# A four-layer graph network: degree norms moved to running totals, own rows added on VectorE, relation products with features on partitions

## The reference, cut to what matters

```
# layer 1: relation weights
xw   = einsum('ni,rio->rno', h, weight)            # 8 relations
msgs = relu(xw[edge_type, src] + bias)
out  = segment_sum(msgs, dst)
# layer 2: two of these, then two dense layers
xw   = h @ W                                        # (A+I): own row included
norm = dis[row] * dis[col]                          # dis = rsqrt(degree of the target side)
agg  = segment_sum(xw[row] * norm[:, None], col) + b
```

## Time and profile before

| | us |
|---|---|
| three runs, median | 9220.77 |
| three runs, lowest and highest | 9168.85, 9257.79 |
| the profiled execution: its own time | 9174.45 |
| the profiled execution: its span | 9172.8 |

### The profile page before, as it was taken

How to read it: one execution, slowest core, us unless ns; L and a number is a source line. 1 busy time by engine, 2 the same in 40 slices (tenths; PEclk the granted TensorE clock), 3 DMA queues, 4 the chain that set the end, 5 groups by cost and what they waited for, 6 DMA issues and landing times. The chain is left out here.

```text
span 9172.8 us, 117781 instructions
## 1 busy us (share of the span) xinstructions
PE 4151.0 (45%) x22767; PEld 3257.0 (36%) x22767; DVE 5226.7 (57%) x22501; ACT 2665.3 (29%) x6456; POOL 4913.5 (54%) x4624
## 2 busy tenths in 40 slices
PE   7004555556678888860003689700167523222000
PEld 1003333336667777760002578600056411111000
DVE  8766555559975666658861467522146544444544
ACT  0670000027632222223321356400022333333222
POOL 0007888864445555555557720166687355555466
PEclk9556665568877888885555799855589755555555
DMA  8893222248832222226654789611279522222333
GB/s 231 325 352 65 41 41 41 41 96 274 276 106 62 64 65 67 65 72 160 161 144 159 236 287 310 200 45 44 63 240 318 193 81 83 80 81 82 94 113 103
DMA packets 1124322, 1274.86 MB, mean 139 GB/s; under 512 B 220752, under 2 KB 933434, under 8 KB 1113735
## 3 DMA queue, kind: packets, MB, share of 16 engines
q1 hardware_dynamic: 924340, 976.35, 33.2%
q0 software_dynamic: 199904, 297.70, 13.6%
HBM read 680.87 MB, written 620.27 MB: 142 GB/s over the span
## 5 line engine op out<-in xcount | busy, mean ns | idle before, releaser
L627 POOL DMA_INDIRECT dense<-t_xs,gidx x784 | 764.9, 976 | 845.1 <-DVE gidx L1388 447.6
L1687 PE MATMUL ps<-w,dense 128*128 128x128 f32 x6272 | 976.4, 312 | 131.0 <-issue 128.4
L1687 PEld LDWEIGHTS ps<-w,dense 128*128 128x128 f32 x6272 | 868.9, 218 | 206.0 <-issue 167.2
L455 POOL DMA_INDIRECT g<-t_src,gidx x398 | 404.4, 1016 | 774.2 <-DVE keyr L489 653.2
L1408 DVE SCALAR_TENSOR_TENSOR dense<-xT 128x256 f32<-128x256 f32 x1568 | 543.9, 418 | 474.4 <-ACT xT L1843 336.4
L627 POOL DMA_INDIRECT dense<-t_y,gidx x392 | 373.3, 952 | 753.0 <-DVE gidx L1498 634.1
L473 POOL DMA_INDIRECT t_acc<-tot,sidx x392 | 641.1, 1635 | 141.8 <-issue 124.2
L757 ACT ACTIVATE dense<-dense,nbi,sc 128x128 f32<-128x128 f32 (+1 forms) x1580 | 624.7, 480 | 232.8 <-DVE nbi L1362 166.7
L1073 POOL DMA_INDIRECT g<-out_rows,gidx x392 | 371.0, 946 | 493.2 <-DVE didx L1544 363.6
L532 PE MATMUL ps<-ident,keyr 128*128 128x128 f32 x394 | 118.6, 399 | 1051.9 <-DVE seq L502 547.8
L565 POOL DMA_INDIRECT out_rows<-dense,sidx x392 | 384.8, 982 | 280.5 <-DVE dense L1593 167.8
(11 more groups left out here) (296 smaller groups left out, 12909.3 us busy)
## 6 DMA issues: line engine op xcount, KB each, us to landing
dense<-t_xs SPq DMA_DIRECT2D x78, 1320.0 KB
dense<-in_x SPq DMA_DIRECT2D x156, 640.0 KB
t_xs<-dense SPq DMA_DIRECT2D x98, 528.0 KB, 7.3
t_xs<-hb SPq DMA_DIRECT2D x78, 660.0 KB
t_sum<-dense SPq DMA_DIRECT2D x98, 512.0 KB
t_src<-dense SPq DMA_DIRECT2D x78, 640.0 KB
t_acc<-dense SPq DMA_DIRECT2D x78, 640.0 KB
dense<-t_acc SPq DMA_DIRECT2D x78, 640.0 KB
```

Source lines behind the costliest of these rows:

```text
L455: gp.indirect_dma_start(rows[:, p.k, c, :], None, table, bass.IndirectOffsetOnAxis(ap=gidx[:, p.k, c:c + 1], axis=0)) \
L627: gp.indirect_dma_start(rows[:, p.k, c, :], None, table, bass.IndirectOffsetOnAxis(ap=gidx[:, p.k, c:c + 1], axis=0)) \
L1687: i = nc.tensor.matmul(ps[:, o:o + P], xm[:, p.w, k, c * P:(c + 1) * P], w1[:, k, :], start=False, stop=(k == R - 1))
```

## The change

Three parts, and small things that go with them.

1. **E1.** The weights become the stationary side and the masked rows of both tiles move together: eight matmuls of 256 columns a pair. The result has features on partitions, so the bias is a column that ACT adds in its relu. PE then turns the two messages back (`turn_back`, lag 2), and the running totals read them from PSUM. The bias matmuls go.
2. **Layer 2's target norm.** E0 and the start of L0 compute on DVE the degree norm of each edge's target from a scan over run lengths (`normd`), with one small matmul and one square root on ACT. In E2, ACT multiplies every total by it (`e2_scaled`, lag 3) into a ring of its own, which SP stores; `run_sums` then waits for this copy in place of the store.
3. **L2.** DVE adds the own rows to the sums in place of scaling them; PE turns the result with ten transposes a block in place of twenty identity matmuls.
4. In **E3** the lag of the running totals behind the gathers goes from 3 to 5.

```diff
             def e1_sums(p):
-                v.wait_ge(E1["relu"].sem, E1["relu"].after(p.q + 1))
-                run_sums(v, R1, p, tot1, msg[:, p.w, 0, :], msg[:, p.w, 1, :], 2)
+                v.wait_ge(E1["back"].sem, E1["back"].after(p.q + 1))
+                run_sums(v, R1, p, tot1, *[ps[:, BACK[p.w] + c * P:BACK[p.w] + (c + 1) * P] for c in range(2)], 2)
...
             def products(p):
...
+                o = XW + p.w * 512
+                for k in range(R):
+                    i = nc.tensor.matmul(ps[:, o:o + 2 * P], w1[:, k, :], xm[:, p.w, k, :], start=(k == 0),
+                                         stop=(k == R - 1))
+                i.then_inc(E1["xw"].sem, 1)
+
+            def turn_back(p):
+                pe.wait_ge(E1["relu"].sem, E1["relu"].after(p.q + 1))
+                if needed(p.q - 1):
+                    pe.wait_ge(R1["second"].sem, R1["second"].after(p.q - 1))
                 for c in range(2):
-                    o = XW + p.w * 512 + c * P
-                    nc.tensor.matmul(ps[:, o:o + P], ones[0:1, :], b1b[0:1, :], start=True, stop=False)
-                    for k in range(R):
-                        i = nc.tensor.matmul(ps[:, o:o + P], xm[:, p.w, k, c * P:(c + 1) * P], w1[:, k, :],
-                                             start=False, stop=(k == R - 1))
-                i.then_inc(E1["xw"].sem, 1)
-
-            pair_loop(pe, (turn, 0), (products, 1))
+                    o = BACK[p.w] + c * P
+                    i = nc.tensor.transpose(ps[:, o:o + P], msg[:, p.w, c, :], ident[:, :])
+                i.then_inc(E1["back"].sem, 1)
+
+            pair_loop(pe, (turn, 0), (products, 1), (turn_back, 2))
...
             def e1_relu(p):
                 if needed(p.q - 1):
-                    a.wait_ge(R1["second"].sem, R1["second"].after(p.q - 1))
+                    a.wait_ge(E1["back"].sem, E1["back"].after(p.q - 1))
                 a.wait_ge(E1["xw"].sem, E1["xw"].after(p.q + 1))
-                nc.scalar.activation(msg[:, p.w, :, :], pair_of(XW + p.w * 512), ACT.Relu).then_inc(E1["relu"].sem, 1)
+                nc.scalar.activation(msg[:, p.w, :, :], pair_of(XW + p.w * 512), ACT.Relu, bias=b1c[:, :]) \
+                    .then_inc(E1["relu"].sem, 1)
...
+            def e2_scaled(p):
+                a.wait_ge(R2["second"].sem, R2["second"].after(p.q + 1))
+                if needed(p.n):
+                    a.wait_ge(R2["keep"][p.k].sem, R2["keep"][p.k].after(p.n * 16))
+                for c in range(2):
+                    i = nc.scalar.activation(scaled2[:, p.k, c, :], tot[:, p.k, c, :], ACT.Copy,
+                                             scale=normd[:, bass.ds(p.q * 2 + c, 1)])
+                i.then_inc(R2["scaled"].sem, 1)
+            pair_loop(a, (e2_root, 0), (e2_body, 1), (e2_scaled, 3))
...
             def enc_scale(r, u, p):
                 b = r * SLOTS + u
                 v.wait_ge(L2["lda"][u].sem, L2["lda"][u].after(r * 16 + 16))
-                nc.vector.tensor_tensor(ain2[u][0:p], ain2[u][0:p], norm_of(u, p, D), ALU.mult).then_inc(L2["scal"].sem, 1)
+                v.wait_ge(L2["h"].sem, L2["h"].after(b + 1))
+                nc.vector.tensor_tensor(ain2[u][0:p], ain2[u][0:p], hb[u][0:p, :, 0:D], ALU.add).then_inc(L2["scal"].sem, 1)
...
                 for k in range(K):
-                    nc.tensor.matmul(ps[:, k * P:k * P + p], ain2[u][0:p, k, :], ident[0:p, 0:p], start=True, stop=False)
-                    i = nc.tensor.matmul(ps[:, k * P:k * P + p], hb[u][0:p, k, 0:D], ident[0:p, 0:p], start=False, stop=True)
+                    i = nc.tensor.transpose(ps[:, k * P:k * P + p], ain2[u][0:p, k, :], ident[0:p, 0:p])
                 i.then_inc(L2["tr"].sem, 1)
...
-            pair_loop(v, (e3_ring, 0), (e3_sums, 3))
+            pair_loop(v, (e3_ring, 0), (e3_sums, 5))
```

```diff
+            nc.vector.tensor_scalar(ta[:, 1:T], cont[:, 1:T], 1.0, None, ALU.mult)
+            chain(nc.vector.memset(ta[:, 0:1], 1.0))
+            v.wait_ge(C0["turned"].sem, C0["turned"].after(2))
+            chain(nc.vector.tensor_copy(carried[:, 0:1], ps[:, 7 * 512:7 * 512 + 1]))
+            chain(nc.vector.tensor_tensor_scan(tb[:, :], ta[:, :], hcol[0][:, :], carried[:, 0:1], ALU.mult, ALU.add))
+            nc.vector.tensor_scalar(normd[:, :], tb[:, :], 1.0, None, ALU.add).then_inc(C0["v"].sem, 1)
+            v.wait_ge(C0["root"].sem, C0["root"].after(2))
+            chain(nc.vector.reciprocal(normd[:, :], normd[:, :]))
```

More of the change, by code:

```diff
@@ L307, in gnn @@
         TURN = (1 * 512, 4 * 512)
+        BACK = (0, 3 * 512)
         SUMS = 2 * 512
@@ L417, in gnn @@
         E0 = phase("edge", NPAIR, EN + "hot count", GA, EXTRA)
-        C0 = phase("target_degrees", 1, "v close root made shared turned carried keys kept")
+        C0 = phase("target_degrees", 1, "v close root made shared turned keys kept")
         SW = {"keep": [16 * len(range(k, NPAIR, RING)) for k in range(RING)]}
@@ L423, in gnn @@
                    {"ld": slots(16), "lda": slots(16), "sto": slots(16)})
-        E1 = phase("edge", NPAIR, "ring bn mv var std rs nb h tx txc masked xw relu", GP)
+        E1 = phase("edge", NPAIR, "ring bn mv var std rs nb h tx txc masked xw relu back", GP)
         R1 = phase("runs", NPAIR, "first second", SC)
@@ L428, in gnn @@
         E2 = phase("edge", NPAIR, "ring joined bn mv var std rs sc nb h", GP)
-        R2 = phase("runs", NPAIR, "first second", SW)
+        R2 = phase("runs", NPAIR, "first second scaled", SW)
         Z2 = phase("last_runs", 1, "made close total last:16")
@@ L640, in run_sums @@
             width = in0.shape[-1]
-            if needed(p.n):
+            if free == "scaled":
+                if needed(p.q - RING + 1):
+                    v.wait_ge(s["scaled"].sem, s["scaled"].after(p.q - RING + 1))
+            elif needed(p.n):
                 v.wait_ge(s[free][p.k].sem, s[free][p.k].after(p.n * (32 if per else 16)))
@@ L907, in keep_runs2 @@
             def keep_runs2(p):
-                sp.wait_ge(R2["second"].sem, R2["second"].after(p.q + 1))
+                sp.wait_ge(R2["scaled"].sem, R2["scaled"].after(p.q + 1))
                 sp.dma_start(t_run2[0:T * P, :].rearrange("(p t) f -> p t f", t=T)[:, bass.ds(p.q * 2, 2), :],
-                             tot[:, p.k, :, :]).then_inc(R2["keep"][p.k].sem, 16)
+                             scaled2[:, p.k, :, :]).then_inc(R2["keep"][p.k].sem, 16)
             pair_loop(sp, (clear(t_yacc, zrow[:, :, 0:H2], E2["h"]), 0), (keep_runs2, 1))
@@ L1304, in needs @@
                 vec.tensor_scalar(need[:, :], needf[:, :], 1.0, None, ALU.max)
+                chain(vec.memset(hcol[0][:, :], 1.0))
+                chain(vec.tensor_tensor_scan(normd[:, :], cont[:, :], hcol[0][:, :], 0.0, ALU.mult, ALU.add))
             def e0_between(pair):
@@ L1344, in _ @@
             v.wait_ge(C0["made"].sem, C0["made"].after(late[0] + 3))
+            late[0] += 3
             for n in range(2):
@@ L1446, in e2_sums @@
                 v.wait_ge(E2["h"].sem, E2["h"].after(p.q + 1))
-                run_sums(v, R2, p, tot, g[:, p.k, 0, :], g[:, p.k, 1, :], 0, "keep")
+                run_sums(v, R2, p, tot, g[:, p.k, 0, :], g[:, p.k, 1, :], 0, "scaled")
             run_start(v, Z2, tot)
             pair_loop(v, (e2_ring, 0), (e2_stats, 3), (e2_scales, 4), (e2_sums, 5))
-            run_close_vector(v, Z2, msg[:, 0, 0, :], D)
+            v.wait_ge(Z2["close"].sem, Z2["close"].after(1))
+            nc.vector.tensor_scalar(msg[:, 0, 0, :], ps[:, SUMS:SUMS + D], carried[:, 1:2], None, ALU.mult) \
+                .then_inc(Z2["total"].sem, 1)
             end_phase(v, VE)
@@ L1661, in conv0_mm @@
                 i.then_inc(L0["mm"].sem, 1)
+            nc.tensor.matmul(ps[:, 7 * 512:7 * 512 + 1], carry[:, :], normd[:, T - 1:T], start=True, stop=True) \
+                .then_inc(C0["turned"].sem, 1)
             node_loop(pe, (conv0_turn, 0), (conv0_mm, 1))
@@ L1703, in enc_turn @@
                 pe.wait_ge(L2["scal"].sem, L2["scal"].after(b + 1))
-                pe.wait_ge(L2["h"].sem, L2["h"].after(b + 1))
                 if needed(b):
@@ L1828, in conv0_first @@
                 relu_rows(a, p, ob_h[u], xin[u], sc[:, u, :], nbi[:, u, :]).then_inc(L0["h"].sem, 1)
+            a.wait_ge(C0["v"].sem, C0["v"].after(2))
+            nc.scalar.activation(normd[:, :], normd[:, :], ACT.Sqrt).then_inc(C0["root"].sem, 1)
             node_loop(a, (conv0_first, 0))
```

20 lines of the change are left out of this document (13 added, 7 removed).

## The result

Beside the kernel before in the same set of runs, the kernel after takes 8843.74 us (median of 4, 8766.52 to 8885.96) against 9194.81 (median of 4): ratio 0.9603, 95% interval 0.9512 to 0.9693. The forecast, 8760 us and faster by over 1%, came true in its total. By the medians the gain is 351 us; the profiled execution of after is the fastest of its four, and beside it the gain is 408 us. The parts of the forecast did not come true, and a later set of runs took the kernel before down to 8050 us. So there are two questions: where the 408 us between the two profiled executions (9174.45 and 8766.52) came from, and when they exist at all.

The account below looks back on a forecast made before the run. E1 was held by PE at 5.23 us a pair plus 455 us lost, mainly to slow stretches, L2 by DMA transfers from block 22. 9174.45 - 290 - 90 - 50 + 3 = 8747, given as 8760 us; range 8520 to 9110.

Parts of the forecast that it names:

- The floor of E1: E1: POOL's gathers and writes set 5.3 us a pair, 1060 us undisturbed, no gain on 1045 by itself.
- E1, -290: E1: 1060 us undisturbed plus 150 us of remaining loss gives 1210, minus 290 us (ends -420 and -40).
- a third of the loss: E1: of the loss to PE's slow stretches, between 20 and 400 us, 150 us was let stand.
- the first rival: The slow stretches vanish: E1 1080 us (-420), L2 -175, E3 -60, total 8522 us; chance 0.25.
- hidden at full clock: E1: DVE's wait for `turn_back` costs nothing, 3.7 + 0.3 us of PE against 5 us of DVE.
- L2, -90: L2: fewer PE records help only the first blocks; middle taken between nothing and at most 180 us.
- E3, -50: E3: the longer lag covers 5 us more of late gathers; minus 50 us, between none and 80.
- full recovery: E3: the upper bound of the longer lag's gain, 80 us, with POOL's floor at 2.49 us a pair.
- E2, +3: E2, L0, E0 and start together +3 us; E2's scaled copies hidden, its store about +1 at the end.
- Clock in L2: L2: transposes may bring PE to 1.2 GHz, a block 10.9 us over DMA's 9.67, +80, 8840 us; chance 0.06.
- Slower, POOL never pausing: E1: POOL hardly pauses, PE keeps crawling at 29.6 us a pair; 26 such pairs give 9317 us; chance 0.08.
- Density of PE's records: E1 and L2: stretches follow PE records per us; E1 from 7.6 to 4.2, L2 6.8 to 3.7, near L3's 3.4.

Follow-up runs that it names:

- E0: Not a run but a phase of the kernel, in which DVE waits for POOL's writes; it takes 1308 us in quiet and disturbed sets.
- quiet sets: Sets of runs in which the kernel before took 8050 and 8052 us with a spread of 0.3%; near variants of after took 0.05 to 0.24% more.
- the second set: After and before, both unchanged, run once more: after 8855.63 us, before 9146.01, ratio 0.9741.
- before_third: The kernel before, unchanged, profiled again in a later set where before took 8965.93 us; its L2 took 984 us, its first six blocks 79.
- disturbed: Said of sets of runs in which the kernel before took 8966 to 9195 us with a spread of about 1% or more.
- e1_narrow: After with E1's products again as sixteen matmuls of 128 columns, thirty-two records: 8056.99 us, ratio 1.0010 to before; once more 8064.29 us.
- pauses: After with small POOL copies between indirect DMAs in E1 and E3, and L2's identity matmuls back: 8860.34 us, ratio 0.9859 to before.
- three: After with E1's totals nine pairs back, L2's identity matmuls back and E3's totals three pairs back: 9073.68 us, ratio 1.0027 to before.

## Why the forecast was right in its total, by luck, and wrong in its parts

- **The floor of E1** (5.3 us a pair by POOL, 1060 us undisturbed): right; quiet sets have 1061 to 1064. PE's 4.5 us a pair at full clock came as well (860.86 / 196 = 4.4 at clock 0.99). That the smaller PE work gains nothing by itself fits the totals of the quiet sets; before's own E1 was not profiled in one.
- **E1, -290; measured -189.** The step that failed: "a third of the loss" to remain, all of it stretches. The stretches vanished from E1 altogether, as the first rival had it, but that rival's 1080 us did not come. The step "hidden at full clock" for the wait of `turn_back` failed: it counts with PE's 3.7 + 0.3 us and takes a signal to arrive when the work ends. With a signal held up to 6.8 us the wait costs DVE 270.6 us, within the 0.3 to 3 us a pair that I had for its cover gone (1.4). Before had held signals as well; I read its 567.1 us of POOL's idle time as the work of stretches alone, and didn't ask what "remote" was in ACT's row. Which part of the edit took the stretches away (fewer records, the weights as the stationary side, the bias matmuls gone) no run shows.
- **L2, -90; measured -202 and, in the second set, -125.** That the pace is bound by transfers was right. That the first blocks crawled and no longer do is right as a description of the two profiles: the first six give 172 us. That fewer PE records end the crawl is not shown: before_third has none with all its records and takes 984 us, and the two runs with the identity matmuls back take 967 and 1026, as after does. The term was mis-sized too: I took the middle between nothing and 180 us, and even that bound was passed by 22 us.
- **E3, -50; measured -7.** The step that failed is "full recovery": it takes every microsecond of DVE's wait for gathers as won. The wait fell from 165.4 to 28.1 us, and DVE's unexplained idle time rose from 233 to 365. Lag 3 or 5 is the same in quiet sets (499) and nearly so in disturbed ones. The floor of 2.49 us a pair was right; quiet sets have 499 us, 2.5 a pair.
- **E2, +3; measured +6 to +10** in the two sets with both kernels, 667 to 671 us in quiet ones, as before's disturbed 668. **L3**, left alone, took 732 and 734 us after and 745 to 805 before; no run explains that. That is 18 of the 408 us, which I had at nothing.
- **Clock in L2** (a rival at 8840): the granted clock fell from 0.98 to 0.85, the price did not come, since PE has 0.28 of the time to spare. The Trainium skill ("TensorE: Matmul & The Clock Gate", Part 4, PE-mode transpose) says that the full clock does not engage for transposes; the trace agrees so far that the full clock is granted less. In quiet sets it is 0.83 to 0.85 with transposes and 0.97 to 0.99 with the identity matmuls; but PE also does less then, and no run parts the two.
- **Slower, POOL never pausing:** its mechanism, loss that grows when POOL pauses less, is the one that the runs come nearest to (lag 9: 1458 us, beside 1304 and 1305 in other sets), though it strikes ACT and DVE, through held signals, and not PE through crawling. In after itself POOL still ran dry often enough (255.8 us).
- **Density of PE's records** as the cause of stretches: not shown. Disturbed E1s had 209, 186 and 144 such records before, 0 and 6 after; but e1_narrow, which would have told density from the swap of sides, met only quiet sets, and L2 gave no clear answer.

The total came out right, 408 us for 427, because E1 gave 101 and E3 43 us less and L2 112 more; phases that I had at nothing make up the rest. That the errors cancel is luck. The step from the profiled execution to the median was off as well: 8747 + 46 is 8793, I gave 8760, and the median is 8844. It was also right only for the condition in which before was profiled; nothing in the text asked whether the stretches were the kernel's or the moment's.

## What to carry to other kernels

Look at "issue" and "remote" before pricing an engine: where both are large while POOL issues indirect DMAs back to back, the time may belong to a disturbance, and a gain there should be measured again in another set before it is believed. Slack for a late signal helps only if it doesn't let POOL run on: a short piece of other work on POOL between pairs of indirect DMAs took the held signals away. And before pricing a loss that no wait explains, as the crawl of L2's first blocks, profile the same kernel again: here a second and third profile of before had L2 at 1152 and 984 us.

## What the hardware showed that I had not expected

- The kernel before takes 8050 us in one set of runs and 9195 in another, 14% more. By phase, after's variants in quiet sets against after: E1 1062 and 1305 us, E3 499 and 571, the scores' phase 1004 and 1282, the last phase, which writes the output rows, 498 and 593, L0 596 both times. What suffers issues indirect DMAs on POOL, but not all that does so suffers: E2, with 392 of them, takes 667 and 674, E0, with 784, 1308 both times. E2's rows are nearly all of two (178 of them in after), as in `pauses`. E0 has a row of 706 and is the exception: there the DMAs start 1.9 us apart at the median, and 1.3 elsewhere.
- In a disturbed set PE's signals are held while POOL's indirect DMAs follow at 1.3 us. L1702's late ones are let go at a median of 1.2 us behind the end of the last in after, and of 1.7 us in `three`. A few small copies on POOL behind every two DMAs leave one late signal of 184. In quiet sets hundreds of DMAs follow less than 0.5 us apart and none of L1702's signals is held. What is behind the disturbance was not found.
- In it single steps of a sequencer take 0.7 us in place of 0.04, on DVE in E3, in clusters; 0.7 us is also the spacing of PE's records in its slow stretches.
